# A two-layer transformer kernel: Newton steps and token mixing spread over more ticks of the schedule

## The reference, cut to what matters

```python
x = x + 0.5 * L0_ffn(layernorm(x))     # token mixing, then gates
x = x + L0_attn(layernorm(x))          # chunked linear attention, 16 heads of 16
x = x + 0.5 * L0_ffn(layernorm(x))
x = x + 0.5 * L1_ffn(layernorm(x))     # base projection + routed low-rank update
x = x + L1_attn(layernorm(x))          # rotary causal softmax attention, 16 heads
x = x + 0.5 * L1_ffn(layernorm(x))

# L0_ffn
xr = mu_r * x + (1.0 - mu_r) * x_prev  # x_prev: the token before
xk = mu_k * x + (1.0 - mu_k) * x_prev
out = sigmoid(xr @ W_r.T) * (relu(xk @ W_k.T) ** 2 @ W_v.T)
# L0_attn, the key norm per head
k = (k - mean(k)) / sqrt(mean((k - mean(k)) ** 2) + EPS)
```

## Time and profile before

| | us |
|---|---|
| median of 3 runs | 2963.05 |
| lowest, highest | 2957.84, 2965.12 |
| profiled execution | 2963.63 |
| its span | 2961.9 |
| TensorE busy (matmul) | 2640.6 |
| VectorE busy | 1862.2 |
| ScalarE busy | 1230.0 |
| GpSimd busy | 754.6 |
| mean granted TensorE clock | 0.93 |

### The profile page before, as it was taken

One profiled execution on the slowest core, in us unless ns is written; L12 is line 12 of the kernel. 1 busy time (PEld: TensorE's weight loads), 2 busy tenths in 40 slices (PEclk: granted clock), 3 DMA queues, 4 the chain that ended last, 5 costly groups with the idle time before them and its releaser, 6 DMA issues.

```text
span 2961.9 us, 45503 instructions
## 1 busy us (share of the span) xinstructions
PE 2640.6 (89%) x15278; PEld 1740.0 (59%) x15278; DVE 1862.2 (63%) x5534; ACT 1230.0 (42%) x2802; POOL 754.6 (25%) x1283
## 2 busy tenths in 40 slices
PE   4885899899999999899999999989998999998986
PEld 3563666456655666466665666556664666555644
DVE  5544667666677567666667666675676666766642
ACT  1321244444444444444444444444444444444452
POOL 2321232223222232223322232222322233211111
PEclk8996899989999999999999899999999999999998
DMA  2015103411333113411134113331134121443211
GB/s 59 1 46 134 23 17 80 115 41 25 70 91 98 39 41 82 129 49 45 38 96 123 40 27 68 93 95 45 35 78 123 52 52 23 100 119 76 64 38 47
DMA packets 137423, 193.97 MB, mean 65 GB/s; under 512 B 49439, under 2 KB 111214, under 8 KB 127854
## 3 DMA queue, kind: packets, MB, share of 16 engines
q1 hardware_dynamic: 131808, 190.89, 25.9%
q10 hardware_dynamic: 5390, 0.18, 0.1%
HBM read 122.34 MB, written 67.63 MB: 64 GB/s over the span
## 4 chain that ended last, share of the span: by engine, by line
PE 71%; DVE 16%; DMA 4%; issue 3%; ACT 3%; POOL 2%; SPq 1%; DVEq 0%; ACTq 0%; POOLq 0%
PE bank L765 9%; PE bank L784 9%; PE bank L750 8%; PE bank L587 5%; PE bank L678 4%; PE bank L518 4%; PE bank L567 4%; PE bank L527 3%; PE bank L536 3%; PE bank L692 3%; DVE bank L1104 3%; PE bank L622 2%; PE bank L497 2%; PE bank L633 2%; PE bank L561 2%
## 5 line engine op out<-in xcount | busy, mean ns | idle before, releaser
L1310 ACT ACTIVATE pexp<-bank 128x512 f32<-128x512 f32 (+3 forms) x1536 | 675.8, 497 | 555.1 <-PE bank L765 554.9
L1104 DVE CUSTOM_DVE_ANT_0 bank<-bank,maskneg 128x256 f32<-128x256 f32 (+3 forms) x1024 | 484.9, 511 | 294.1 <-PE bank L750 291.5
L765 PE MATMUL bank<-stq,stk 128*128 128x512 f32 (+3 forms) x1536 | 558.6, 435 | 58.0 <-ACT pexp L1310 54.9
L750 PE MATMUL bank<-stk,stq 128*128 128x512 f32 (+3 forms) x1536 | 512.8, 399 | 100.1 <-DMA stk<-k_halves 31.3
L765 PEld LDWEIGHTS bank<-stq,stk 128*128 128x128 f32 x1536 | 274.5, 200 | 344.3 <-ACT pexp L1310 210.4
L1107 DVE TENSOR_REDUCE mxa<-bank 128x1 f32<-128x512 f32 x512 | 348.7, 685 | 133.2 <-PE bank L750 128.4
L1458 POOL TENSOR_SCALAR_AFFINE_SELECT pexp<-pexp 128x256 f32<-128x256 f32 x512 | 214.3, 425 | 743.0 <-ACT pexp L1310 742.6
L750 PEld LDWEIGHTS bank<-stk,stq 128*128 128x128 f32 x1536 | 288.2, 203 | 184.5 <-issue 120.6
L784 PE MATMUL bank<-pexp,vsm 128*32 128x512 f32 (+3 forms) x3072 | 360.9, 544 | 5.7 <-POOL pexp L1458 5.5
L1376 POOL TENSOR_SCALAR_AFFINE_SELECT arena<-arena 128x512 f32<-128x512 f32 x128 | 78.5, 638 | 416.3 <-ACT arena L1212 416.3
L587 PE MATMUL bank<-arena 32*128 32x256 f32 x1024 | 158.0, 428 | 17.2 <-DVE arena L911 14.2
(11 more groups left out here) (186 smaller groups left out, 4204.3 us busy)
## 6 DMA issues: line engine op xcount, KB each, us to landing
stq<-q_halves SPq DMA_DIRECT2D x128, 256.0 KB
arena<-rope_table SPq DMA_DIRECT2D x8, 2048.0 KB
q_halves<-arena SPq DMA_DIRECT2D x32, 512.0 KB, 3.0
k_halves<-arena SPq DMA_DIRECT2D x32, 512.0 KB, 2.8
stk<-k_halves SPq DMA_DIRECT2D x64, 256.0 KB
stk<-k_halves SPq DMA_DIRECT2D x128, 128.0 KB
v_rows<-arena SPq DMA_DIRECT2D x16, 544.0 KB, 4.1
vsm<-v_rows SPq DMA_DIRECT2D x16, 544.0 KB, 3.8
```

The source lines that it names most:

```text
L750: last = mm(bk[:, col:col + n], stq[b_][:, h % 2, qb * P:(qb + 1) * P], stk[b_][:, h % 2, k0:k0 + n], start=True, stop=True)
L765: mm(ps(j)[:, 0:n], stk[b_][:, j, kb * P:(kb + 1) * P], stq[b_][:, j, (c + 1) * CH - n:(c + 1) * CH], start=True, stop=True).then_inc(s["t ...
L1104: last = nc.vector.tensor_tensor_reduce(out=sc, in0=sc, in1=maskneg[:, CH - n:CH], scale=1.0, scalar=LOWEST, op0=ALU.add, op1=ALU.max, acc ...
L1310: nc.scalar.activation(pexp[:, u % NPX, j, 0:n], ps(j)[:, 0:n], ACT.Exp, scale=DK ** -0.5).then_inc(s["exp_done"], 1)
```

## The change

- The Newton iterations of the key norm stand on three ticks, one each (`rsqrt` becomes a generator with a `yield` behind each iteration). `lin` is 32 ticks instead of 30, in all queues.
- The four mixing operations of an FFN stand on four ticks, one each, 6 to 9. An FFN is 15 ticks instead of 14.
- A front is then 95 ticks instead of 91. In the words given with the change it is three ticks; by the diff, the steps up to the second FFN move by three and those behind it by four.
- `SX` goes from 129 to 132 core steps (3.75 ticks), the tails' starts go 4 ticks later, and SP's steps of a front by 3 and then 4.

```diff
-        SX = 129
+        SX = 132
...
-        G_AT = [FT * (b + 3) for b in range(NB - 2)] + [1014, 1134]
+        G_AT = [FT * (b + 3) + 4 for b in range(NB - 2)] + [1018, 1138]
...
                 def ffn_pe(c, b, f):
                     yield from ln_pe(c, b, 2 * f, xns)
-                    yield from idle(2)
+                    yield from idle(3)
...
                         last.then_inc(s["f_full"], 1)
                         yield
-                    yield
+                    yield from idle(3)

                     def scores(j, half):
...
                             nc.vector.scalar_tensor_tensor(out=xm[:, :, k], in0=xv(c)[:, k].rearrange("p (h t) -> p h t", h=2),
                                                            scalar=mu[:, m, 0, k:k + 1], in1=xm[:, :, k], op0=ALU.mult,
                                                            op1=ALU.add).then_inc(s["mix"][c], 1)
-                        yield
-                    yield from idle(4)
+                            yield
+                    yield from idle(3)
...
                         then(nc.vector.scalar_tensor_tensor(out=y, in0=tmp, scalar=1.5, in1=y, op0=ALU.add, op1=ALU.mult))
+                        yield
...
-                    rsqrt(krf, kvf, ktf, s["newton"][c], NEWTON * b + 1)
-                    yield
+                    yield from rsqrt(krf, kvf, ktf, s["newton"][c], NEWTON * b + 1)
...
                     yield
-                    yield from idle(2)
+                    yield from idle(3)

                     def relu(h):
...
                         nc.scalar.copy(khT[:, k], f_bank(c, b, "khT", k)).then_inc(f_freed(c, b, "khT", k), 1)
                         yield
+                    yield from idle(2)
...
-                    yield from idle(8)
+                    yield from idle(9)

                 def lin_pool(c, b):
...
-                    yield from idle(7)
+                    yield from idle(9)

                     def spread_heads(j):
...
                 def front_sp(c, b):
                     sp = nc.sync
-                    yield from idle(52)
+                    yield from idle(55)
...
-                        yield from idle(7)
+                        yield from idle(8)
                     else:
-                        yield from idle(25)
+                        yield from idle(26)
```

## The result

The changed kernel takes 3002.15 us, median of 4 runs (2999.52 to 3004.84), against 2964.09 us for the kernel before, timed beside it. The ratio is 1.013, with a 95% interval of 1.0108 to 1.0151. It is 38 us slower, where I had forecast 16 us faster. 3002 lies outside the range of 2915 to 2976. A few executions of a kernel can fall in a slower state of the chip and are left out of the ratios; here that is one of e5, at 2991.83 us.

The account below looks back on a forecast made before the run. The kernel was taken as bound by TensorE's instructions in written order, plus its waits. Terms 1 to 4, -5 - 12 + 3 - 2 = -16 us, gave 2963 - 16 = 2947 us; whole range 2915 to 2976 us.

Parts of the forecast that it names:

- the paragraph on SP's queue: SP's transfers: rope issue from tick 70 to 73, its user from 76 to 80, so the transfer stays covered; no loss.
- the light ticks: Slower rival: TensorE lacks front work on ticks 28, 29, 51, 52, so its clock may fall; 2976 us, chance 0.19.
- Term 1: Batch 1: half of 5.36 us of VectorE waits goes, with part of the half clock; gain 5 us.
- Term 2: Repeated batches 2 to 7: fewer VectorE waits at routing and chunk 1's zone, 2 us each; gain 12 us.
- no change: Rival: the costly waits are ScalarE's and VectorE's only move to another burst; 2960 us, chance 0.27.
- Term 3: ScalarE's waits beside the Newton sequences: chunk 0's 2.16 us stay, chunk 1's grow by 0.46; loss 3 us.
- Term 4: The start: batch 1's first transposes fall into the first score's wait of 17.98 us for its stack; gain 2 us.
- the larger gain: Rival: waits beside both Newton sequences go, and their half clock with them; 61 us faster, 2902 us, chance 0.10.

Follow-up runs that it names:

- e5: The changed kernel with SP's rope step behind the stack load, Newton sequence on three ticks, but mixing on two ticks again; 2965.57 us, ratio 1.0009.
- e1: The changed kernel with SP's rope step one tick later, so the stack load is again ahead of the rope transfer; 2939.39 us, ratio 0.9933.
- e2: The kernel before with only SP's rope step one tick earlier, so it stands ahead of the stack load; 3019.96 us, ratio 1.0203.
- e6: The kernel before, fronts of 91 ticks, nothing stretched or moved, with only Newton and mixing spread over ticks; 2945.22 us, ratio 0.9931.
- e9: The changed kernel with only SX = 131 in place of 132; 2932.78 us, ratio 0.9888.
- e11: The changed kernel with the rope transfer issued from ScalarE's queue and SP's stack load held until after that issue; 3012.31 us, ratio 1.0161.

## Why the prediction was wrong, point by point

**The step that failed** is the paragraph on SP's queue. It compared the rope step with its user ("both 7 or more ticks by 2.9 us, so the transfer stays covered") and gave "the first stack load by 3.75", but it never put the rope step and the stack load of the middle of a batch side by side. They shared a tick; the rope step moved by 3 and the load by 4, and the load then stood behind 2 MB. e1 and e2 show it with one tick in either kernel: 63 and 58 us. The comparison that the paragraph did make was off too: 70 to 76 is 6 ticks, 17 us at 2.9 us a tick, less than the 22.32 us that this transfer takes in the chain of batch 0 before. VectorE waits for it in that trace, 6.0 us in all, 6 times; that is small and has no part in the loss. I also had no slower rival of this kind; the one I had, the light ticks at 2976 us, has another cause, and e1 speaks against it: it has the same light ticks and is faster than the kernel before.

The trace after prices the collision: seven waits of 4.1 to 5.6 us are some 36 us, and the rest is TensorE running longer on the same work. Between the profiled executions of the changed kernel and of e1 the span differs by 54.3 us, TensorE's idle time after 300 us (the window less its busy time) by 29.4 (256.4 less 227.0) and its busy time over the whole span by 25.3 (2642.9 less 2617.6, same 15278 instructions). In windows of 2 us each of the seven waits has a stretch of 4 to 12 us with a lowered clock on it, down to 0.50; what the clock lacks of full speed in these seven adds up to 23 us. That is the half clock that comes with each wait.

**The sum without it was close, in part by luck.** -16 us were forecast; e1 gives -23 and e6 -18 against their kernels before. But the parts of the sum do not match. Timed from one k_halves transfer to the next in the profiled executions, e1 against before: the end of front 0 is 2.4 us later, batch 1 takes 3.2 us less (304.7 against 307.9), the six repeated batches together 29.1 us less (2023.3 against 2052.4, where terms 2 and 3 had 9), and from the last front to the end it takes 11.6 us more, where the sum had nothing. A gain that was put too low and a loss that was left out partly cancel. In the changed kernel the same three stretches are 6.9, 10.0 and 13.8 us longer than before, and the end of front 0 is 5.2 us later.

Term 1, batch 1: half of 5.36 us was to go. After, the two waits behind VectorE's scores are 3.30 and 1.11 us, 4.4 in place of 5.4, and the one for the masking is gone from there; but 0.33 us behind a score follow, and a masking later in the batch is waited for 1.72 us, where nothing stood before. A gain of at most 1 us and not 2.7; "under 3 us together" did not come. With the clock, e1 has the 3.2 us above, of 5 forecast. In e6, too, 1.23 and 2.95 us stand there.

Term 2: the VectorE rows were to fall. The two that I named did, from 35.0 to 26.4 us, as forecast (32.1 in e1). But mxb's row on the same line, which I had left out as small, went from 5.7 to 17.1 (18.4 in e1). L750's three rows were 40.7 in all, are 43.5 after and 50.5 in e1 (20.6, 18.4 and 11.5). Taken together the term has the wrong sign: VectorE's waits moved to other scores and did not go. That is what the "no change" rival had said of them.

Term 3: ScalarE's waits were to stay or grow. They fell from 44.3 to 23.9 us, and 27.1 in e1. The 2.16 us of chunk 0's zone are gone: after, the `tscore` on that tick follows without idle time. In chunk 1's zone 0.45 us are left, with 1.07 us behind VectorE:

```profile
1084.64 0.47 PE L750 MATMUL bank<-stk,stq 128*128 128x512 f32 x1 [1.07 <-DVE mxa L1104]
1085.92 0.98 PE L765 MATMUL bank<-stq,stk 128*128 128x512 f32 x2 [0.45 <-ACT pexp L1311]
```

I had put 0 for chunk 0's zone and a loss for chunk 1's, by adding up ScalarE's operations between two exponentials. Why the gap closed no run shows; that TensorE reaches these ticks at another moment relative to ScalarE is my reading.

Term 4, the start: the first score waits 4.54 us in place of 17.98, and the transposes of batch 1 stand ahead of it, with 11.46 us of waiting for VectorE of their own. The two waits are 16.0 us, 2.0 less, as forecast. But the end of front 0, where k_halves goes out, is 5.2 us later in the chain (276.17 against 271.02), outside the 2 us that I had allowed for it, so the start lost. e1 has 273.4.

The period was to be 346 us in place of 348.0. Over the last three batches it is 347.1 in the changed kernel, 341.1 in e1 and 348.2 before.

**Where the gain came from** is therefore mostly the clock and not the idle rows. From before to e1 TensorE's idle time after 300 us rose (218.3 to 227.0 us), and its busy time fell by 23.0 us (2640.6 to 2617.6) for the same instructions; the mean granted clock went from 0.930 to 0.936. In e9 it is 0.944 and 2594.6 us. These are single profiled executions, but the clock of all timed ones agrees: its median is 0.937 in e1 (7 executions) and 0.9315 in the kernel before (16). Summed over windows of 2 us after 300 us, what the clock lacks of full speed comes to 159 us before, 169 after, 138 in e1 and 113 in e9. Why the clock stays up longer in e1 is not shown.

The section of the Trainium skill that I weighed ("TensorE: Matmul & The Clock Gate", "A second HAM failure mode: psum-queue depth-cycling") would have had frequent short idle moments pull the clock down. In e1 TensorE's waits for VectorE on line 750 are more (78 of 0.65 us mean against 54 of 0.75 us, with mxb's 18 counted before), and the clock is higher. But its waits for ScalarE are fewer (30 against 48), and with them the two kernels have 108 and 102. So the number of short waits does not tell the clock here, for the rule or against it. What the traces show is that the clock fell with single longer waits, as with the 5.57 us above.

**What stays open.** After the last front the changed kernel needs 344.4 us to the end, the kernel before 330.6. No rope transfer falls there, and e1 needs 342.2. e9, with the same fronts and tails and only the core one step earlier, needs 331.1 (its span of 2920.3 less the start of this piece), while the other kernels with `SX` = 132 need 339.5 to 345.8. So the loss at the end is not the longer fronts':

```profile
2589.18 2.77 DMA k_halves<-arena
```

What the start of the core at step 132 collides with there was not found. In this stretch of the changed kernel the clock is low around the tail of sequence 6, where it was higher before (windows):

```profile
2794.00:2808.00 14.00, 12.10 (x52) 0.51 0.02 4
2820.00:2830.00 10.00, 8.27 (x35) 0.66 0.07 15
```

The corresponding stretches of before have 0.88 and 0.83. That accounts for up to 7 of 13.8 us. The load at each batch's end also waits longer (2.85 us against 1.92 in batch 4), behind a k_halves transfer of 3.80 us in place of 2.82. These were not tried by themselves.

One sum of the prediction was off without effect: the larger gain took 17 us for terms 1, 2 and 4, which by their own sizes are 16 (5, 9 and 2, with the earlier trace rows already counted).

## What to carry to other kernels

When steps of a static order are moved by "about the same" amount, list for each queue the neighbours of every DMA before and after, the small ones that somebody waits for above all. The distance from a transfer to its own user is not enough: a transfer that nobody waits for can delay one that is waited for. Where the order of two issues is left to a tie between ticks, write it down as an order. And a kernel timed as slower may hold a gain that one misplaced issue hides: here 63 us of loss on 23 us of gain.

## What the runs showed of the hardware

A stack load whose last piece lands about 6 us after its issue elsewhere (6.15 us in the chain of the changed kernel) took 27.8 us when the 2 MB rope transfer had been issued 3.2 us ahead of that piece from the same queue, and 24.1 us when it had been issued 5.2 us ahead from ScalarE's queue: 31.1 and 29.3 us from the issue of the rope transfer, which takes 22 us where nothing collides. Whether another queue would let the load pass was open before e11. The Trainium skill ("Trainium Kernel Development and Optimization", section "Key Constraints") says that the queues of SP, ACT and POOL all run on the same 16 DMA engines and interleave, so that issuing from several saves only the sequencer's issue time; e11 agrees, and shows that interleaving did not let the small load through early.

TensorE's busy time for the same 15278 matmuls was 2642.9, 2640.6, 2617.6 and 2594.6 us in the changed kernel, the one before, e1 and e9. A busy time is no constant of the work; it carries the clock, and a gain can sit there with more idle time beside it.
